# One 3 KB row per pixel between the two phases of a convolution and spiral-scan kernel, and a pointwise product on split operands

## What is computed

```python
h = relu(x)                                    # x: (32, 56, 56, 256) f32
h = conv(h, dw_kernel, rhs_dilation=(2, 2), feature_group_count=256) + dw_bias
h = conv(h, pw_kernel) + pw_bias               # 1x1
h = h * inv + (beta - moving_mean * inv)       # inv = gamma * rsqrt(var + eps)
for ci, ni, nm, nc in spiral_path:             # 3136 steps
    neigh = (h[:, ni] * nm).sum(1) / nc        # 4 neighbours, present values
    y = tanh(concat(h[:, ci], neigh) @ w1 + b1) @ w2 + b2      # w1: 512 x 512
    h[:, ci] = h[:, ci] + y * w_y
```

## Time and profile before

| | |
|---|---|
| median of 3 runs | 4759.45 us (4752.06 to 4760.44) |
| the profiled execution | 4755.92 us, its span 4754.1 us |
| PE busy | 4491.0 us, 94% |
| DVE busy | 3981.0 us, 84% |
| POOL busy | 3445.8 us, 72% |
| ACT busy | 2551.0 us, 54% |
| moved by DMA | 835.52 MB in 394994 packets |
| phase one | 0 to about 3174 us (last store of sums issued at 3171) |
| phase two | about 3174 to 4754 us |

### The profile page before, as it was taken

The page is one execution under the profiler, slowest core; times in us unless marked ns, Lnnn a source line. Parts: engine busy times, 40 slices in busy tenths (PEclk is TensorE's granted clock), DMA queues, the critical chain, the costliest instruction groups (busy, mean ns, idle before and its releaser), DMA issues.

```text
span 4754.1 us, 62034 instructions
## 1 busy us (share of the span) xinstructions
PE 4491.0 (94%) x19609; PEld 3350.7 (70%) x19609; DVE 3981.0 (84%) x5685; ACT 2551.0 (54%) x4523; POOL 3445.8 (72%) x2478
## 2 busy tenths in 40 slices
PE   4999999999999999999999999998888899999889
PEld 3888878888888888888878888864444445555556
DVE  7888888888888788888888888738888888898884
ACT  4566656666666666665656666444344444444552
POOL 1888888888887788888888888756666666665542
PEclk8999999999999999999999999999999999999999
DMA  4344444444444444444444444359999998888751
GB/s 101 124 139 134 133 134 140 132 135 138 131 138 138 129 138 134 131 142 131 132 132 140 132 136 130 151 178 318 303 299 320 296 301 291 287 273 256 209 176 51
DMA packets 394994, 835.52 MB, mean 176 GB/s; under 512 B 76848, under 2 KB 178480, under 8 KB 394544
## 3 DMA queue, kind: packets, MB, share of 16 engines
q1 hardware_dynamic: 249008, 417.52, 31.4%
q0 software_dynamic: 143408, 411.26, 23.2%
q10 hardware_dynamic: 2256, 2.77, 0.2%
HBM read 420.17 MB, written 425.85 MB: 178 GB/s over the span
## 4 chain that ended last, share of the span: by engine, by line
PE 61%; DVE 12%; issue 10%; ACT 7%; DMA 5%; POOL 4%; SPq 0%; DVEq 0%; POOLq 0%; ACTq 0%
PE psum L888 13%; PE psum L890 13%; PE psum L889 13%; PE psum L872 13%; DVE psum L752 5%; DMA out<-dw_rows 4%; DVE dw_rows L760 3%; ACT relu_rows L563 3%; POOL out L476 3%; PE psum L861 3%; PE psum L928 2%; PE psum L912 1%; PE psum L901 1%; DMA s_pre<-eo,wave_idx 1%; PE psum L919 1%
## 5 line engine op out<-in xcount | busy, mean ns | idle before, releaser
L676 DVE SCALAR_TENSOR_TENSOR dw_rows<-relu_rows,taps,dw_rows 128x1792 f32<-128x1792 f32 x872 | 1803.4, 2079 | 6.2 <-issue 5.2
L464 POOL DMA_INDIRECT s_pre<-eo,wave_idx x784 | 1327.0, 1693 | 249.7 <-issue 224.2
L458 POOL DMA_INDIRECT s_x<-xo,wave_idx x784 | 1215.2, 1550 | 377.5 <-issue 233.8
L476 POOL DMA_INDIRECT out<-dw_rows x897 | 899.8, 1003 | 677.2 <-issue 401.3
L888 PE MATMUL psum<-w_hi,u_hi 128*128 128x512 f32 x3136 | 1383.4, 441 | 0.0
L890 PE MATMUL psum<-w_hi,u_lo 128*128 128x512 f32 x3136 | 1231.8, 393 | 0.0
L889 PE MATMUL psum<-w_lo,u_hi 128*128 128x512 f32 x3136 | 1224.7, 391 | 0.0
L517 ACT ACTIVATE eo<-psum 128x512 f32<-128x512 f32 x784 | 468.1, 597 | 1218.6 <-PE psum L890 1160.9
L901 PE MATMUL psum<-dw_rows,ident 128*128 128x512 f32 x1666 | 885.0, 613 | 98.1 <-DVE near L752 74.7
L872 PE MATMUL psum<-pw,dw_rows 128*128 128x256 f32 x3136 | 818.8, 384 | 61.6 <-ACT psum L572 44.9
L581 ACT ACTIVATE psum<-psum 128x512 f32<-128x512 f32 x897 | 522.0, 582 | 545.8 <-PE psum L912 283.7
(11 more groups left out here) (90 smaller groups left out, 3913.6 us busy)
## 6 DMA issues: line engine op xcount, KB each, us to landing
dw_rows<-s_pre SPq DMA_DIRECT2D x615, 256.0 KB
x_tok<-x SPq DMA_DIRECT2D x112, 896.0 KB
dw_rows<-s_x SPq DMA_DIRECT2D x615, 128.0 KB
dw_rows<-s_pre SPq DMA_DIRECT2D x169, 192.0 KB
dw_rows<-s_x SPq DMA_DIRECT2D x169, 96.0 KB
out<-dw_rows POOLq DMA_INDIRECT x897
s_x<-xo,wave_idx POOLq DMA_INDIRECT x784
s_pre<-eo,wave_idx POOLq DMA_INDIRECT x784
```

The source lines that it names most:

```text
L458: pool.indirect_dma_start(s_x, bass.IndirectOffsetOnAxis(wave_idx[:, n:n + 1], 0), xo[:, n % XO_SLOTS, :], None, bounds_check=TILES * P - ...
L464: pool.indirect_dma_start(s_pre, bass.IndirectOffsetOnAxis(wave_idx[:, n:n + 1], 0), eo[:, n % EO_SLOTS, :], None, bounds_check=TILES * P - 1,
L476: pool.indirect_dma_start(out_rows, bass.IndirectOffsetOnAxis(store_idx[:, c:c + 1], 0), o_t[:, c % OUT_SLOTS, :], None, bounds_check=OUT_ ...
L676: dve.scalar_tensor_tensor(out=dst, in0=pair_rows(relu_rows, k + ky - 1, c, 2 * kx * NB), scalar=taps[:, c, 3 * ky + kx:3 * ky + kx + 1], ...
```

## The change

1. The two intermediate arrays become one: `ex` holds a tile's sums and pixels side by side (768 numbers), POOL scatters it once per tile as rows of 3 KB (one indirect transfer where there were two), and the scan's slots `px_t` hold both.
2. The intermediate array in HBM is two arrays, one for each half of the images. A scan tile's partitions are ordered half, ring, image instead of ring, image. SP issues two loads of 64 partitions x 3 KB per tile (one per half) instead of one of 128 x 2 KB and one of 128 x 1 KB.
3. There are 14 such slots. SP waits for the slot by the finished pixel of the tile 14 before; the semaphore `passed` is gone. Output slots go from 4 to 6 and live, with the small tables, in `x_tok`'s memory.
4. The pointwise product moves from its own place at the tick's start to the sums' tile, 6 ticks later, and takes their split operands: `pw` is split into `pw_hi` and `pw_lo`, and for the two blocks that hold the pixel three f32r products of 128x256 follow the products of 128x512 with the same stationary operand, 6 a tile. The ACT copy of the pixels follows that of the sums.
5. Clearing the slots (`memset` of all 14) and the loads of the small tables wait for `lo_ready` and `x_transposed` instead of `xp_ready`.

The core of the diff:

```diff
-PRE_SLOTS, XT_SLOTS, OUT_SLOTS, BANKS, AHEAD = 6, 8, 4, 6, 4
+PX_SLOTS, OUT_SLOTS, BANKS, AHEAD = 14, 6, 6, 4
+HP = P // HALVES
...
-            for n in range(TILES + X_BEHIND):
-                c = n
-                if c < TILES:
-                    q0, q1 = held(c)
-                    if c >= PRE_SLOTS:
-                        back = c - PRE_SLOTS
-                        sp.wait_ge(copied if by_act(back) else passed, handed(back, by_act(back)))
-                    sp.dma_start(pre_t[B * q0:B * q1, c % PRE_SLOTS, :],
-                                 s_pre[c * P + B * q0:c * P + B * q1, :]).then_inc(pre_in[c % PRE_SLOTS], 16)
...
+            for c in range(TILES):
+                q0, q1 = held(c)
+                if c >= PX_SLOTS:
+                    sp.wait_ge(out_ready, c - PX_SLOTS + 1)
+                for h in range(HALVES):
+                    sp.dma_start(px_t[HP * h + NB * q0:HP * h + NB * q1, c % PX_SLOTS, :],
+                                 s_px[h][c * HP + NB * q0:c * HP + NB * q1, :]).then_inc(px_in[c % PX_SLOTS], 16)
...
-                n = tick - ROW_AT - 2
+                n = tick - ROW_AT - TILE_LAG - 2
                 if 0 <= n < TILES1:
                     pool.wait_ge(xp_copied, n + 1)
-                    pool.indirect_dma_start(s_x, bass.IndirectOffsetOnAxis(wave_idx[:, n:n + 1], 0),
-                                            xo[:, n % XO_SLOTS, :], None, bounds_check=TILES * P - 1,
-                                            oob_is_err=False).then_inc(x_stored[n % XO_SLOTS], 16)
-                n = tick - ROW_AT - HID_LAG - 2
-                if 0 <= n < TILES1:
                     pool.wait_ge(hid_copied, n + 1)
-                    pool.indirect_dma_start(s_pre, bass.IndirectOffsetOnAxis(wave_idx[:, n:n + 1], 0),
-                                            eo[:, n % EO_SLOTS, :], None, bounds_check=TILES * P - 1,
-                                            oob_is_err=False).then_inc(e_stored[n % EO_SLOTS], 16)
+                    pool.indirect_dma_start(s_px[n // (H * T)], bass.IndirectOffsetOnAxis(wave_idx[:, n:n + 1], 0),
+                                            ex[:, n % OUT1_SLOTS, :], None, bounds_check=TILES * HP - 1,
+                                            oob_is_err=False).then_inc(stored[n % OUT1_SLOTS], 16)
...
-                    for c in range(CK):
-                        last = pe.matmul(bank, dw_rows[:, R % D_SLOTS, c, NB + P * t:NB + P * (t + 1)], pw[:, c, :],
-                                         start=False, stop=c == CK - 1, skip_group_check=True)
-                    last.then_inc(xp_ready, 1)
...
+                        pe.matmul(hid, hi, w_hi[:, k, :], start=k == 0, stop=False)
+                        if k < CK:
+                            pe.matmul(point, hi, pw_hi[:, k, :], start=False, stop=False, skip_group_check=True)
+                        pe.matmul(hid, hi, w_lo[:, k, :], start=False, stop=False)
+                        if k < CK:
+                            pe.matmul(point, hi, pw_lo[:, k, :], start=False, stop=False, skip_group_check=True)
+                        last = pe.matmul(hid, lo, w_hi[:, k, :], start=False, stop=k == 2 * CK - 1)
+                        if k < CK:
+                            last_point = pe.matmul(point, lo, pw_hi[:, k, :], start=False, stop=k == CK - 1,
+                                                   skip_group_check=True)
```

More of the change, by code:

```diff
@@ L33 @@
 ROW_AT = 21
-HID_LAG = 6
+TILE_LAG = 6
 FIRST_TICK = -20
@@ L108, in by_act, with handed @@
     return live(SEQ[c][0]) == 2
-def handed(c, who):
-    return sum(by_act(i) == who for i in range(c + 1))
+def handed(c):
+    return sum(by_act(i) for i in range(c + 1))
 def part_of(level, g):
@@ L182, in shape_tables @@
                 g2, q2 = at_group[r2]
-                rows = slice(B * q2, B * (q2 + 1))
+                rows = q_of == q2
                 if t == 8 * r - 1 and i2 == 0:
@@ L325, in build @@
         gam, bet, mme, mva, pwb_r, inv = (su_near.take(C) for _ in range(6))
[L326 to L332, removed]
+        pw_t = su_ex.take(CK * C).rearrange("p (k n) -> p k n", k=CK)
+        b1_r = su_ex.take(HID)
+        be = su_ex.take(HID)
+        cst, t0 = (su_ex.take(C) for _ in range(2))
+        cst_b = su_ex.take(CK * P).rearrange("p (k n) -> p k n", k=CK)
+        wy_b = su_ex.take(CK * P).rearrange("p (k n) -> p k n", k=CK)
+        wy_s, t1 = (su_ex.take(C) for _ in range(2))
         tmp_r = u_hi[:, 0, 0:2, :]
+        pw = relu_rows[:, R_SLOTS - 1, :, PADX * NB:PADX * NB + C]
         x_in = [sem(f"x_in{i}") for i in range(X_SLOTS)]
@@ L349, in build @@
         hid_copied = sem("hid_copied")
-        x_stored = [sem(f"x_stored{i}") for i in range(XO_SLOTS)]
-        e_stored = [sem(f"e_stored{i}") for i in range(EO_SLOTS)]
+        stored = [sem(f"stored{i}") for i in range(OUT1_SLOTS)]
         tabs_in = sem("tabs_in")
@@ L357, in build @@
         v_ready = sem("v_ready")
-        pre_in = [sem(f"pre_in{i}") for i in range(PRE_SLOTS)]
-        xt_in = [sem(f"xt_in{i}") for i in range(XT_SLOTS)]
-        passed = sem("passed")
+        px_in = [sem(f"px_in{i}") for i in range(PX_SLOTS)]
         copied = sem("copied")
@@ L566, in _ @@
                                    ACT.Relu).then_inc(row_ready, 1)
-                n = tick - ROW_AT - 1
+                n = tick - ROW_AT - TILE_LAG - 1
                 if 0 <= n < TILES1 - XP_BANKS:
@@ L728, in _ @@
                                       ALU.subtract).then_inc(lo_ready, 1)
-            dve.wait_ge(xp_ready, TILES1)
-            for i in range(PRE_SLOTS):
-                last = dve.memset(pre_t[:, i, :], 0.0)
-            last.then_inc(pre_clear, 1)
+            dve.wait_ge(lo_ready, 4 * ROWS)
+            dve.memset(pre_t, 0.0).then_inc(pre_clear, 1)
             dve.wait_ge(hid_ready, TILES1)
```

119 lines of the change are left out of this document (51 added, 68 removed).

## The result

Four runs of the changed kernel gave 4547.01 to 4565.45 us, median **4558.31**; four of the kernel before, measured with them, 4752.06 to 4760.44, median 4757.8. The ratio is 0.958 (0.9556 to 0.9604): 4% faster. The forecast of 4584 us is 26 us high, and inside its range.

A forecast was written before the change was run, and what follows sets the result against it. PE was taken to bound phase one, with ACT one tick in seven; transfers the scan at 7, 6 and partly 5 groups, PE and DVE at 4. 4755.9 - 106 (phase one) - 66 (scan) = 4584 us, range 4495 to 4700.

The forecast's parts named there:

- Product: Phase one on PE: six 128x256 f32r products at 0.12 us each replace 0.86 us; a tile takes 3.48 us.
- Rival A: Phase one: weight loads show in short products, 0.188 us each, making the kernel slower at 4864 us; chance 0.07.
- ACT's tick: Phase one: one tick in seven is set by ACT's order and falls only from 3.96 to 3.85 us.
- One scatter: Phase one: POOL goes from 3.84 us a tile to at most 1.82 + 0.30; worth nothing by itself.
- Rival C: Phase one stays near 27.3 us a row, held by DVE or ACT; only the scan gains, 4690 us; chance 0.10.
- Row length: Scan loads: 122 fewer packets a tile at 18.9 ns each save 0.144 us of DMA work a tile.
- Depth: Scan: loads of sums start 9 tiles ahead instead of about 2, so PE's waits for transfers should nearly vanish.
- Output slots: Scan: slots rise from 4 to 6, so the 34.5 us wait for earlier output transfers should nearly vanish.
- Next bound: Scan: DVE at a 0.92 share limits next, 1.45 us a tile with 7 groups; the scan gains 66 us.
- the signs set ahead: Both phases: observations named beforehand as right, such as a row near 26.4 us and a scan tile under 1.50 us.
- B: Scan: DMA is priced by bytes, so nothing is gained there and the time is 4650 us; chance 0.17.
- E: Whole kernel: 64-partition loads or 3 KB rows cost what was saved; within 10 us of before; chance 0.02.

The follow-up runs named there:

- e11: The kernel before with 6 output slots in place of 4 and nothing else; 4618.08 us (0.9722).
- e9: The changed kernel with the two halves on alternate partitions instead of 64 adjacent ones, still one load per half; 4510.22 us (0.9494).
- e7: The changed kernel with one scan load of 128 rows of 3 KB a tile, all from the first half's array (other pixels); 4506.32 us (0.9489).
- e6: The changed kernel with scan loads of 128 rows in two transfers, 2 KB and 1 KB pieces, from the first half's array (other pixels); 4510.44 us (0.9497).
- e10: The changed kernel with 4 output slots in place of 6; 4672.88 us (0.9835).
- e1: Phase one of the kernel before (f32 pointwise product, two scatters, rows 4 KB apart) with the changed kernel's scan; 4698.95 us (0.9889).
- e2: The changed kernel with each tile's row sent by two scatters again, rows 4 KB apart; 4749.5 us (0.9989).
- e3: The changed kernel with ACT's refill of the pixel bank moved ahead of u_hi and the relu; 4499.7 us (0.9478).
- e8: The changed kernel, one scatter, with the pixel product back in f32 on u_hi alone, without the part of u_lo; 4651.47 us (0.9808).
- e4: The kernel before with ACT's refill of the pixel bank moved earlier and nothing else; 4813.52 us (1.0137).

## Why the prediction was right, and where it wasn't

Time from the first output scatter to the end of the profiled execution:

| kernel | us | edit against before |
|---|---|---|
| before | 1567.7 | |
| e11 | 1433.3 | 6 output slots |
| e9 | 1434.7 | and depth, 3 KB rows, one row per pixel, halves interleaved |
| e7 | 1434.0 | as e9 with one load of 128 rows |
| e6 | 1439.2 | as e7 in pieces of 2 KB and 1 KB |
| after | 1493.2 | as e9, halves of 64 adjacent partitions |
| e10 | 1604.5 | as after, 4 output slots |

The kernels that share after's scan or nearly so (e1, e2, e3, e8) have 1478 to 1504 us here, so the adjacent halves cost 45 to 70 us by this table and 48 by the medians. The scan's 74.5 us are then -134 for the output slots, about 0 for the rest of the new layout, and +48 to +60 for the adjacent halves. The forecast had -66 for row length and depth. With 4 output slots (e10) the new layout's scan is 37 us longer than before's. That the forecast's number for the scan came near is luck.

- **Product: right.** s, the price of a 128x256 product, measured 0.11 to 0.12, the row 26.4. The step from the halved row of 128x512 to 128x256 held. Rival A would have made the distance 0.188. The Trainium skill's page TensorE: Matmul & The Clock Gate (Part 3) has a weight load overlap a running matmul only when the row group differs; the trace doesn't agree, with 0.11 to 0.12 between products of the full array that each reload their weights.
- **ACT's tick: right.** (3.85 - 3.48) x 112 = 41 us is what I left in the row for it; taking it away gave 58.6 (e3), so it was sized low: the pause and the slow first product behind it come to 0.52 us a row, not 0.37.
- **One scatter: wrong as a term.** "Worth nothing by itself" is nearly so (14 us, e8). But "a POOL with 0.07 us to spare" was read as room. Its waits for ACT, 24 us of 1000 in the earlier trace rows, were all the room there was, and e2 shows POOL full at 3.97 us a tile: a faster PE gains nothing without the merge. Rival C had POOL near full as a point for it, in a kernel where POOL's load had just been halved; it belonged to the question of which edit carries the gain.
- **Row length: wrong.** The 18.9 ns came from a line through two queues of different kinds, loads and scatters, as if size were their only difference. It measured 4.75, e6 against e7 on one queue. By the estimate of 3.5 ns from the Trainium skill's page DMA: Bandwidth & Descriptors ("Why small descriptors are slow (HBM only)") the term is 0.027 us a tile; e6 and e7 agree with its order in the packet's price (4.75 ns by the shares); of the time that it would give, 24 us over 897 tiles, they show 4 in all. I had named it and set it aside for my own rows.
- **Depth: wrong.** The lead of before was about 6 tiles, not 2; only the place where the slot is given back had to be followed in the code. With the depth of before e11's scan is as short as e9's, so the added depth brought nothing that shows.
- **Output slots: the mechanism named, its size missed.** One half sentence had it, as a wait that should vanish. It is the whole gain of the scan. The step that failed was calling DMA the bound on a share of 0.94: with the same rows and loads e11 moves 371 GB/s, not 309, at a share of 1.03.
- **Next bound: wrong.** DVE doesn't stop at 0.92; e11 and e9 have 301.63/314 and 265.93/278 = 0.96, the far end of my range. The change as it stands has 0.88, held by its loads. So of the signs set ahead, the short products, the row, POOL near half and the tile under 1.50 us came; a DMA share at or under 0.94 (1.03) and DVE over 0.9 (0.88) did not, and they were the ones that tested the reason.
- **Rivals.** B (4650) had the right reason, that long rows save next to nothing, and the wrong sum, since the slots' gain was under no term. E had the adjacent halves, at 0.02, only as a thing that would eat all the gain.

What stays open: why 6 slots of output give just what they do (8 was not tried), by what step e4's earlier refill lengthens the scatters, why e1's phase one is 19 us longer, and why the unchanged scan varies from 1478 to 1504 us.

## What to carry to other kernels

Before pricing what an engine or a queue saves, find which buffer's release the next instruction waits for: two more slots were worth about 61 us in a stretch of 364 where the wait's row named 34.5, because everything behind the waiting instruction stood too. An engine that is nearly full isn't off the path, it is the ceiling of any edit that speeds up the one ahead of it; such edits have to be tried as a pair (e2, e8). And take a transfer's price from two rows of one queue that differ in size alone.

## What the runs showed of the hardware

*A load onto 64 adjacent partitions is slower than one onto 64 alternate ones.* After against e9: 336 and 373 GB/s (372 in the very same stretch), 48 us in the kernel, with the same number of loads, rows and bytes a tile. The Trainium skill's page SBUF — State Buffer ("Door 1: The DMA port swizzle") lets bit 6 of the partition number choose one half of the ports, so that such a load would reach 8 of 16. The measured difference agrees in kind; no run here shows the ports.

*On POOL, an indirect transfer often lasts until 0.85 us after the DVE instruction beside it has ended.* The timeline of the kernel before, 1005 to 1032 us (rows of other instructions left out):

```profile
1007.35 0.97 POOL L458 DMA_INDIRECT s_x<-xo,wave_idx  x1 [0.30 <-issue]
...
1009.03 1.23 DVE L726 TENSOR_TENSOR u_lo<-near,u_hi 128x1024 fp32r<-128x1024 f32 x1 [2.83 <-issue]
...
1028.24 2.07 DVE L676 SCALAR_TENSOR_TENSOR dw_rows<-relu_rows,taps,dw_rows 128x1792 f32<-128x1792 f32 x1
1029.37 1.79 POOL L458 DMA_INDIRECT s_x<-xo,wave_idx  x1 [0.30 <-issue]
...
1031.38 2.07 DVE L676 SCALAR_TENSOR_TENSOR dw_rows<-relu_rows,taps,dw_rows 128x1792 f32<-128x1792 f32 x1
1031.47 2.83 POOL L464 DMA_INDIRECT s_pre<-eo,wave_idx  x1 [0.30 <-issue]
```

While DVE is idle (2.83 us ahead of 1009.03) a transfer takes 0.97 us. Beside L676 it takes until L676 ends and 0.85 us more: 1030.31 + 0.85 = 1031.16 = 1029.37 + 1.79, and 1031.38 + 2.07 + 0.85 = 1034.30 = 1031.47 + 2.83. From 1000 to 1400 us there are 206 scatters; 161 of them last over 1.05 us, and 146 of these end within 0.03 us of 0.85 behind the end of L676, L689, L702 or L726, all of them DVE instructions with two inputs in SBUF. So the same scatter costs 1 to 3 us by where it falls. That would explain why two of them fill POOL and why a mere shift (e4) changes their price. It doesn't always happen: the scatter at 1008.63 takes 0.97 us with L726 starting beside it at 1009.03. And not every DVE instruction does this: in the scan DVE is busy for 0.88 of the time, and a scatter takes 224.31/220 = 1.02 us. This is read from coincidences in the trace; no run took DVE's work away. The Trainium skill's page SBUF — State Buffer ("SBUF: two separate sides") has GpSimd wait for descriptor writes until DVE gives back a shared port; the part of that section on a bandwidth-pool intuition gives some 0.115 us behind DVE's end. These rows agree in kind, with 0.85 us.
